# A fused Mamba and FFN block on one core: the hand-laid steps of a chunk changed, one more VectorE tile, a GpSimd product that is no longer in place, and a bias that comes from columns

## The reference, cut to what matters

```python
mod = (_silu(c) @ wmod).reshape(2, 6, 1, -1)        # sa, ca, ga, sb, cb, gb
h = _layernorm(x) * (1 + ca) + sa
x = x + ga * mamba(h)
h = _layernorm(x) * (1 + cb) + sb
x = x + gb * ((h @ factors.sum(0)) / sqrt(8) + bias)
# mamba: E = 1024 channels, N = 16 states
h, gate = split(h @ in_proj); h = silu(conv4(h) + conv_b)
dt, B, C = split(h @ x_proj); dt = softplus(dt @ dt_proj + dt_b)
s[t] = s[t-1] * exp(dt[t] * A[n]) + dt[t] * h[t] * B[t, n]   # for each channel and each n
y[t] = sum over n of s[t, n] * C[t, n] + h[t] * D
out = (y * silu(gate)) @ out_proj
```

## Time and profile before

| | |
|---|---|
| Time, median of 3 runs | 2000.46 us (1999.31 to 2001.25) |
| The profiled execution | 2002.29 us, of which the span of its instructions is 2000.6 |
| Busy: PE, DVE, ACT, POOL | 1794.8, 1811.3, 1548.5, 1825.4 us |
| Granted TensorE clock over the span | 0.944 of full speed |

### The profile page before, as it was taken

One profiled execution on the slowest core, in us unless ns is written; L12 is line 12 of the kernel. 1 busy time (PEld: TensorE's weight loads), 2 busy tenths in 40 slices (PEclk: granted clock), 3 DMA queues, 4 the chain that ended last, 5 costly groups with the idle time before them and its releaser, 6 DMA issues. The chain is left out here.

```text
span 2000.6 us, 29195 instructions
## 1 busy us (share of the span) xinstructions
PE 1794.8 (90%) x9096; PEld 1337.8 (67%) x9096; DVE 1811.3 (91%) x2232; ACT 1548.5 (77%) x4501; POOL 1825.4 (91%) x756
## 2 busy tenths in 40 slices
PE   7967988999899898999999899899989999899798
...
GB/s 179 247 116 176 130 22 158 23 142 59 80 116 28 158 22 127 75 56 135 33 133 89 81 141 22 158 23 137 64 80 117 27 158 22 119 57 44 105 27 32
DMA packets 72000, 186.17 MB, mean 93 GB/s; under 512 B 6818, under 2 KB 8482, under 8 KB 63908
## 3 DMA queue, kind: packets, MB, share of 16 engines
...
## 5 line engine op out<-in xcount | busy, mean ns | idle before, releaser
L605 POOL TENSOR_TENSOR ub<-u,b_all 128x2048 f32<-128x2048 f32 x255 | 1167.7, 4579 | 40.3 <-DMA b_all<-bc_scratch 40.3
L759 ACT ACTIVATE decay<-dt,decay_rate 128x256 f32<-128x256 f32 x2048 | 882.3, 465 | 22.4 <-DVE state_p L1522 3.4
L1522 DVE TENSOR_TENSOR_SCAN decay<-decay,ub 128x512 f32<-128x512 f32 x589 | 700.8, 1215 | 32.2 <-ACT decay L759 30.9
L623 POOL TENSOR_TENSOR state_p<-state_p,c_all 128x1024 f32<-128x1024 f32 (+1 forms) x256 | 531.2, 2075 | 92.8 <-ACT carry L745 54.3
L1522 DVE TENSOR_TENSOR_SCAN state_p<-decay,ub 128x512 f32<-128x512 f32 x435 | 512.2, 1209 | 41.1 <-ACT decay L759 40.7
L1093 PE MATMUL y_bank<-ident,sc_d 128*128 128x128 f32 x2356 | 353.5, 282 | 144.0 <-DVE sc_d L1537 143.8
L1093 PEld LDWEIGHTS y_bank<-ident,sc_d 128*128 128x128 f32 x2356 | 277.3, 144 | 233.9 <-DVE sc_d L1537 174.8
L1537 DVE TENSOR_TENSOR sc_d<-decay,c_all 128x512 f32<-128x512 f32 x589 | 380.8, 678 | 42.3 <-PE y_bank L1093 34.7
L745 ACT ACTIVATE carry<-decay 128x2 f32<-128x2 f32 x589 | 96.1, 163 | 270.9 <-DVE sc_d L1537 270.0
L1093 PEld LDWEIGHTS y_bank<-ident,state_p 128*128 128x128 f32 x1740 | 217.2, 149 | 69.0 <-issue 37.6
L1093 PE MATMUL y_bank<-ident,state_p 128*128 128x128 f32 x1740 | 240.7, 286 | 15.1 <-POOL state_p L623 15.0
(11 more groups left out here) (137 smaller groups left out, 1876.7 us busy)
## 6 DMA issues: line engine op xcount, KB each, us to landing
win_h<-win_m SPq DMA_DIRECT2D x128, 256.0 KB, 2.6
win_z<-win_m SPq DMA_DIRECT2D x128, 256.0 KB, 3.0
...
```

Source lines behind the costliest of these rows:

```text
L605: pool.tensor_tensor(ub[:, slot, :, :, :], u[:, (PAIRS * c + q) % U_PAIRS, :, :].unsqueeze(1).to_broadcast([P, QUAD, 2, ROWS]), b_all[:, n ...
L623: pool.tensor_tensor(part, part, c_all[:, n:n + k, :].unsqueeze(2).to_broadcast([P, k, 2, ROWS]), ALU.mult).then_inc(pooled, 1)
L759: last = act.activation(bk[:, j * ROWS:(j + 1) * ROWS], dt[:, pair % DT_PAIRS, j, :], ACT.Exp, scale=decay_rate[:, e, n:n + 1])
L1522: dve.tensor_tensor_scan(dst, bk[:, :], ub[:, quad % UB_RING, i, :, :].rearrange("p j r -> p (j r)"), 0.0, ALU.mult, ALU.add).then_inc(sca ...
```

## The change

There are five parts.

1. The table for POOL's products in chunks 2 to 15 changes from 28 units a chunk to 26: 2 units more are multiplied by DVE. Quads 2, 6 and 14 have one unit fewer on POOL, quad 7 one more.
2. DVE's ring of product tiles has four tiles instead of three.
3. POOL's product is written to a ring `sc_p` of four tiles of its own, and `state_p` shrinks from eight tiles to four. POOL no longer waits until ACT has kept the carry of the units; it waits until PE has turned the quad that used its `sc_p` tiles before. DVE, before it scans into a `state_p` tile, now waits for POOL's product and ACT's carry of the quad that used the tile before, where it used to wait for PE's turn.
4. The FFN's bias is kept as columns, 128 x 4 x 2 (`bias_col`), and put into PSUM by four transposes of broadcast columns. `scale_bias` reads the gate from PSUM, where PE has turned it (`turn_gate`), instead of from two tiles in SBUF. The two small DMAs of the gate are gone.
5. Pieces of the neighbouring chunks are issued at other steps: on ACT `modulate_before`, `skip`, `z_after`, `modulate_after` and `seam_decays`, on PE `expand_dt`, `project_dt`, `project_h`, `project_out` and `project_ffn`, and three small ones on DVE.

```diff
-D_RING = 3
+D_RING = 4
-M_AT = (2, 1)
-IN_AT = ((2, 3, 4, 5, 7, 8, 9, 10), (2, 3, 4, 5, 8, 9, 10, 11))
+M_AT = (2, 2)
+IN_AT = ((2, 3, 4, 5, 7, 8, 9, 10), (1, 3, 4, 5, 8, 9, 10, 11))
-P_RING = 8
+P_RING = 4
-EVERY_POOL = (2, 2, 2, 1) * PAIRS
+EVERY_POOL = (2, 2, 1, 1, 2, 2, 1, 2, 2, 2, 2, 1, 2, 2, 1, 1)
...
-                last = QUAD * quad + on_pool(quad)[-1]
-                pool.wait_ge(scanned, last + 1)
-                pool.wait_ge(carried, carries_after(last))
+                pool.wait_ge(scanned, QUAD * quad + on_pool(quad)[-1] + 1)
+                wait(pool, turned_p, quad_before(quad) + 1)
                 k, slot, n = POOLED[quad], FIRST_SLOT[quad], n + on_pool(quad)[0]
-                part = state_p[:, slot:slot + k, :, :]
-                pool.tensor_tensor(part, part, c_all[:, n:n + k, :].unsqueeze(2).to_broadcast([P, k, 2, ROWS]),
+                pool.tensor_tensor(sc_p[:, slot:slot + k, :, :], state_p[:, slot:slot + k, :, :], c_all[:, n:n + k, :].unsqueeze(2).to_broadcast([P, k, 2, ROWS]),
                                    ALU.mult).then_inc(pooled, 1)
...
                         if s in (25, 29):
                             soft_dt(c + 1, 2 * (s // 29))
                             soft_dt(c + 1, 2 * (s // 29) + 1)
-                    if lc is not None and s == 23:
+                    if lc is not None and s == 24:
                         modulate_after(c - 1, 1)
...
-                        if s == 19:
+                        if s == 20:
                             skip(c + 1, 0)
-                        if s in (27, 31) and (c + 1) % PER:
+                        if s in (26, 31) and (c + 1) % PER:
                             seam_decays(c + 1, s // 31)
...
-                        if s == 21:
+                        if s == 22:
                             z_after(c - 1)
-                        if s == 22:
+                        if s == 23:
                             act.wait_ge(mods_made, 4)
                             modulate_after(c - 1, 0)
...
+            def spread_bias(t, b):
+
+                for k in range(KD):
+                    pe.matmul(bank_c[t][:, k * P:(k + 1) * P], bias_col[:, k, b:b + 1].to_broadcast([P, P]), ident[:, :],
+                              start=(k == 0), stop=False, is_transpose=True, skip_group_check=True)
...
-                pick = ident[0:BATCH, c // PER:c // PER + 1].to_broadcast([BATCH, P])
-                pe.matmul(bank_c[t][:, :], pick, bias_row[:, :], start=True, stop=False)
+                spread_bias(t, c // PER)
...
-                        if s in (22, 23, 26, 27):
-                            expand_dt(c + 1, s - 22 - 2 * (s // 26))
+                        if s == 21:
+                            expand_dt(c + 1, 0)
+                        if s == 22:
+                            expand_dt(c + 1, 1)
...
                         if s == 23:
                             ffn_bias(c - 1, 0)
                             project_ffn(c - 1, 0, (0,))
-                        if s == 24:
+                        if s == 23:
                             project_ffn(c - 1, 0, (1, 2, 3))
...
-                        wait(dve, turned_p, turned_before(quad))
+                        before = quad_before(quad)
+                        if before >= 0:
+                            dve.wait_ge(pooled, before + 1)
+                            dve.wait_ge(carried, carries_after(QUAD * before + on_pool(before)[-1]))
...
-                dve.wait_ge(bias_loaded, 16 * BATCH)
-                dve.wait_ge(bias_gated, 16 * BATCH)
-                dve.scalar_tensor_tensor(out=bias_row[:, :], in0=bias_row[:, :], scalar=math.sqrt(RANK), in1=bias_gate,
+                dve.wait_ge(bias_loaded, 16)
+                dve.wait_ge(gate_turned, 1)
+                dve.scalar_tensor_tensor(out=bias_col[:, :, :], in0=bank_c[0][:, 0:KD * BATCH].rearrange("p (k b) -> p k b", b=BATCH),
+                                         scalar=math.sqrt(RANK), in1=bias_in[:, :].unsqueeze(2).to_broadcast([P, KD, BATCH]),
                                          op0=ALU.mult, op1=ALU.mult).then_inc(bias_scaled, 1)
```

94 lines of the change are left out of this document (55 added, 39 removed).

## The result

The changed kernel takes **1929.38 us** (median of 4 runs, 1927.5 to 1929.91) against 2000.86 (4 runs, 1999.31 to 2002.17): a ratio of 0.9641, 95% interval 0.9625 to 0.9658. That is 71.5 us less, where 32 were forecast.

What follows compares the result with a forecast made beforehand. DVE's instruction stream with its 7.4 us of stops a chunk was taken to set the time. The terms summed to -32.2 us, from 2002.3 to 1970.1; the predicted median was 1969, range 1946 to 1996.

Steps and rivals of the forecast that it cites:

- Steps 21 to 24: ACT's decays ahead of normalization and modulations remove the stops at steps 22 and 23: -13.8 us; PE's place there even.
- The fourth tile: At step 26 DVE's product no longer waits for PE's turn of unit 48, so that stop disappears: -28.7 us.
- Two more products: Two products more on DVE a chunk at 0.64 us each: +17.9 us with chunk 15; POOL's relief worth nothing.
- what of it falls into stops: DVE's extra products take the place of stops: -10.8 us at step 5's tap, -4 behind quads 6 and 14.
- The tap's term: Quad 2's extra DVE product replaces the stop before the convolution tap at step 5: -10.8 us.
- The steady bias: At step 23, four transposes for the FFN bias should take less than 2.07 us; PE's place there called even.
- The first modulation at +3.9: At step 2 both modulations stand by copy_y, where one was: +0.3 us a chunk, +3.9 in all.
- the handshake at 0: New waits among POOL, PE and DVE, least room at quads 6 to 8: cost 0, bounds 0 and +20 us.
- chunks 0 and 1: DVE's shorter bias instruction in chunk 0 gives -1.5 us, POOL being the bound; moved steps in chunk 1 give -2.
- The last chunk: Chunk 15 also gets two more DVE products; the last bias on the path at the end gives -1 us.
- C: More than the sum: PE's clock stays at the upper level, stops at step 25 shrink; 1935 to 1955 us, chance 0.08.
- E: Slower: PE falls back at quads 6 and 7, POOL stops, DVE waits at quad 8; 2005 to 2025, chance 0.10.

Runs made afterwards that it cites:

- c_mat: The changed kernel with both first modulations of a steady chunk back at step 1 and the input projection back from step 2: 1933.06 us, ratio 0.9655.

## Why the prediction was wrong, step by step

**What bounds the kernel: right.** DVE's stream with its stops. The profile after shows nothing but fewer stops.

**The step that failed: "Steps 21 to 24",** with its PE place "even". I counted the two stops that it removes, 13.8, and let 7.8 of it be given back. So the term was -6 net. The moves alone are worth 36 us (1965.5; 34.3 in chunks 2 to 14), and 31 in the new layout. Three things were missing: the stops at steps 20 and 26 that end with the same decays (2.5 and 7.2), the 9.2 us that the stop for PE loses, and the clock. I had read the clock of 0.54 at this very place, and that PE had waited for DVE just before, and then priced PE's work as if that clock were given. Chunks 4 and 11 of the same trace had the counterexample, 117.7 us against 118.9; I looked at chunk 5 alone. The clock is half of the effect or somewhat more in the old layout only; in the new one the moves bring their own stops and those behind them (65.2 us of idle time without them, 42.8 with them). "What is late next" I asked of ACT and PE, but never what is no longer late.

**"The fourth tile": the mechanism right, the worth wrong.** The stop goes to nothing, as said. By itself that gives 13 us of the 28.7, since steps 26 and 29 take the rest. In the kernel that was forecast it gives 0, since two other parts have cured the stop already. The forecast added terms that are alternatives.

**"Two more products" and "what of it falls into stops": wrong sign.** I had 17.9 - 10.8 - 4, +3 in all. Measured, the table is worth -21 (1952.3 to 1931.0). The tap's term held (11.8 to 0). Step 2's stop, which I took for untouched at 7.5, grows to 13.6 with ACT's moves, 20.8 with the columns too, and 22.1 with all other moves, and the table takes 12.9 of it. That part goes through POOL, PE and `copy_y`, and I had given POOL's two units no worth, "since DVE waits for no product of POOL": in the kernel before that was so, and with ACT's stops gone it no longer was. A smaller slip: of the row of 10.8 for the tap, 1.6 stand at step 13 and not at step 5. And the price of a product was too high: two of them take 1.18 us from start to start (734.31 to 735.49 above), so 0.59 and 15.3 in 26, not 0.64; each stop saved also spares about 0.085 us of start that lies under the instruction before when DVE runs through. With 120 stops fewer (224 to 104) these are 10 us. The rest of the forecast rise of 17 is in instructions that are a few ns shorter on average (a product 675 ns instead of 679, a scan into `decay` 1212 instead of 1215). That is why DVE's busy time did not rise.

**The steady bias "even": wrong as a part, nearly right in the whole** (21 us alone, 2 in the new layout). **The first modulation at +3.9: wrong sign** (about -4, c_mat). **PE's moves, the handshake at 0, `scale_bias`, chunks 0 and 1: right** (0, 1.6 within the error, 0.15 us for the instruction, -1.3 and -3.6 against -1.5 and -2). DVE now waits 5.6 us for `ub` in chunk 0, so POOL is the bound there as forecast. **The last chunk: an omission.** It has the new layout too; I had it at +1.3 for products and -1 for the tail, and it gave 7.6.

Of the signs named: DVE's wait for PE gone, the tap's gone, steps 22 and 23 gone, steps 25 and 29 larger (13.4 to 17.1, 6.2 to 8.2), POOL waiting for PE at quads 6 and 7 with 1.6 at most and for no carry, copy_y not longer for PE (42.3). All came true but DVE's busy time. That the total came out at more than twice the forecast is no single term: ACT's moves and the table are some 25 us each beyond their terms and the last chunk 7.6, while the fourth tile gives almost nothing of its 28.7.

The rivals: C came nearest in kind (more than the sum, the clock at its upper level) and had 0.08, but not POOL's part, and its clause that the stops at step 25 shrink is wrong (13.4 to 17.1). E's mechanism is real and 1.4 us of room was indeed thin: with the old table it costs 65 us (2017.4 against 1952.3). It was the table, which I read as work moved to DVE, that keeps it away.

**The sum along one path**, each a run: 2000.9, bias -21, ACT's moves -18, fourth tile -1, the other moves -8, the table -21, out of place -2, 1929.4. In another order the bias would have 4, and ACT's moves 36. These steps set medians of different comparisons side by side, in which the kernel before took 2000.9 to 2008.8, so each is good to a few us at best; the -8 of the other moves is the least certain, since the intervals of its two ratios overlap (5.6 in chunks 2 to 14).
